# Column tiles of 32 for the attention sums of the second stage, a later split of the bias, and weight loads released after the first layer norm

## The reference, cut to what matters

```python
def attn(x, w_qkv, w_proj, b_proj):          # 16 heads of 64, 8 groups
    qkv = grouped_linear(x, w_qkv, None)
    q, k, v = (qkv[0] * D ** -0.5, qkv[1], qkv[2])
    attn = softmax(einsum('bhnd,bhmd->bhnm', q, k))
    out = einsum('bhnm,bhmd->bhnd', attn, v)
    return grouped_linear(out, w_proj, b_proj)

def ffn(x, w_gate, w_up, w_down):
    # _bitlinear: activations quantised to 8 bits per row, weights to -1, 0, 1
    # with the scale 1 / mean(|w|)
    gate = silu(_bitlinear(x, w_gate))
    up = _bitlinear(x, w_up)
    return _bitlinear(gate * up, w_down)

x = _layernorm(x + attn(x, w_qkv, w_proj, b_proj))
x = _layernorm(x + ffn(x, w_gate, w_up, w_down))
```

## Time and profile before

| | us |
|---|---|
| median of 3 runs | 1275.42 |
| lowest, highest | 1275.38, 1419.03 |
| the profiled execution | 1273.93 |
| its span (slowest core, core 7) | 1272.2 |
| spans of the eight cores | 1261.5 to 1272.2 |
| TensorE matmul busy | 1155.9 (91%) |
| VectorE busy | 907.3 (71%) |
| ScalarE busy | 581.4 (46%) |
| GpSimd busy | 232.1 (18%) |

### The profile page before, as it was taken

How to read it: one execution, slowest core, us unless ns; L and a number is a source line. 1 busy time by engine, 2 the same in 40 slices (tenths; PEclk the granted TensorE clock), 3 DMA queues, 4 the chain that set the end, 5 groups by cost and what they waited for, 6 DMA issues and landing times.

```text
span 1272.2 us, 17965 instructions; the slowest of 8 cores (1261.5 to 1272.2 us)
## 1 busy us (share of the span) xinstructions
PE 1155.9 (91%) x6502; PEld 453.8 (36%) x6502; DVE 907.3 (71%) x1748; ACT 581.4 (46%) x644; POOL 232.1 (18%) x236
## 2 busy tenths in 40 slices
PE   2898998886698879999999999999899999999997
PEld 0333332232232223333333333333444444444443
DVE  4788879998798786463746545444789777977774
ACT  2898997885354435554655556563011111111110
POOL 4132137764000862010101010000000000000000
PEclk9999998998898989999999999999999999999999
DMA  8999936699879594231423233110623333232303
GB/s 239 309 315 308 314 136 197 206 317 322 243 207 216 170 270 109 65 78 45 103 62 87 71 71 88 37 36 11 160 81 82 93 90 91 65 90 69 75 34 82
DMA packets 129895, 179.54 MB, mean 141 GB/s; under 512 B 90129, under 2 KB 90897, under 8 KB 129810
## 3 DMA queue, kind: packets, MB, share of 16 engines
q1 hardware_dynamic: 120338, 148.67, 41.6%
q0 software_dynamic: 8896, 29.27, 7.4%
q10 hardware_dynamic: 576, 0.46, 0.1%
HBM read 127.41 MB, written 30.93 MB: 124 GB/s over the span
## 4 chain that ended last, share of the span: by engine, by line
PE 66%; DVE 16%; DMA 8%; issue 4%; POOL 3%; ACT 3%; SPq 0%; POOLq 0%; DVEq 0%; ACTq 0%
PE ps L813 31%; PE ps L908 16%; PE ps L564 6%; PE ps L582 6%; DMA stage<-wu 5%; PE ps L589 5%; ACT P L570 2%; POOL G L434 2%; DVE wgq L450 2%; DVE asum L420 2%; DVE wuq L450 1%; DMA stage<-wd 1%; DMA xqT<-XQ 1%; DVE G L434 1%; DVE h L825 1%
## 5 line engine op out<-in xcount | busy, mean ns | idle before, releaser
L570 ACT ACTIVATE P<-ps 128x1024 bf16<-128x1024 f32 x512 | 493.1, 1023 | 260.7 <-PE ps L564 259.2
L813 PE MATMUL ps<-wgq,xqT 128*128 128x512 fp8e4 x1024 | 248.4, 382 | 26.8 <-DMA xqT<-XQ 17.5
L813 PE MATMUL ps<-wuq,xqT 128*128 128x512 fp8e4 x1024 | 251.7, 385 | 13.9 <-DVE h L825 13.9
L819 ACT ACTIVATE T<-ps,tsc 128x512 f32<-128x512 f32 x128 | 88.2, 689 | 385.0 <-PE ps L813 330.3
L908 PE MATMUL ps<-wdq,hqT 128*128 128x512 fp8e4 x1024 | 228.7, 379 | 0.0
L582 PE MATMUL ps<-P,onesb 128*64 128x512 bf16 x1024 | 206.5, 399 | 11.5 <-DVE DT L605 11.4
L589 PE MATMUL ps<-P,V 128*64 128x512 bf16 x1024 | 200.6, 388 | 1.0 <-DVE U L606 1.0
L564 PE MATMUL ps<-Q,K 64*128 64x512 bf16 x1024 | 175.0, 392 | 26.0 <-ACT P L570 13.2
L813 PEld LDWEIGHTS ps<-wgq,xqT 128*128 128x128 bf16 x1024 | 96.0, 98 | 156.7 <-issue 51.5
L813 PEld LDWEIGHTS ps<-wuq,xqT 128*128 128x128 bf16 x1024 | 96.7, 99 | 147.8 <-issue 42.4
L908 PEld LDWEIGHTS ps<-wdq,hqT 128*128 128x128 bf16 x1024 | 97.6, 98 | 126.0 <-issue 12.8
(11 more groups left out here) (95 smaller groups left out, 741.8 us busy)
## 6 DMA issues: line engine op xcount, KB each, us to landing
stage<-wu SPq DMA_DIRECT2D x64, 512.0 KB, 12.1
stage<-wd SPq DMA_DIRECT2D x58, 512.0 KB, 7.2
stage<-wg SPq DMA_DIRECT2D x42, 512.0 KB, 15.7
XB<-x SPq DMA_DIRECT2D x16, 512.0 KB, 4.6
xp_s<-XB SPq DMA_DIRECT2D x16, 512.0 KB, 2.6
Y<-xp_s SPq DMA_DIRECT2D x16, 512.0 KB, 3.9
y<-Y SPq DMA_DIRECT2D x16, 512.0 KB, 2.7
stage<-xT SPq DMA_DIRECT2D x10, 512.0 KB, 13.8
```

Of the source, the lines that this page charges most:

```text
L570: exp_tok[i] = act.do(lambda e: e.activation(P_sb[i % 4][:, :], bank(sb, 2), AF.Exp, bias=-C0, scale=0.125), pv_tok.get(i - 4), t)
L813: tp = pe.do(lambda e, ic=ic, w=w, bk=bk: e.matmul(bank(bk), xqT[b][:, ic, :], W_sb[w][:, 8 * q + ic, sl], start=(ic == 0), stop=(ic == 7) ...
L819: ta = act.do(lambda e: e.activation(T[:, :], bank(gb), AF.Tanh, bias=0.0, scale=tsc[:, t:t + 1]), tp, T_free[k], sc_tok[t])
```

## The change

1. The second piece of x for the first QKV units goes through the queue of SyncE, second in its order, and no longer through that of ScalarE.
2. The row of the bias is still loaded at the start, but `bias_rows` (the clearing, the five VectorE operations of one row, the two GpSimd DMAs) is emitted at i = 4 of the first stage's loop.
3. From step 256 on, `emit_pv_pair` replaces `emit_pv`. The outputs of a step are made with four matmuls on column tiles of 32 (two halves of each head). The denominators of two steps and two heads are made together with four matmuls on column tiles of 32: one 32-row quarter of bank 5 per head and parity of the step. Two steps take 12 matmuls instead of 8, and the order is outputs, outputs, denominators. `norm` then adds the two parities: four copies 32x16, one addition 128x16, and the reciprocal.
4. The first stage goes on to step 257 (three more rounds of its loop), and the second has 254 steps left.
5. `hold[0]` falls not at i = 230 but as soon as i > 244 and `bg` is empty, so behind `x2` of tile 0. The low credit of 0.3 from i = 242 on ends with it.
6. A limit of the down matrix costs 1.2 in the planner instead of 0.75, and up to three, not two, roundings may stand ahead of their limits.

```diff
-        t_x4[(g, j)] = (act if n == 1 else sp).dma(
+        t_x4[(g, j)] = sp.dma(
...
-    t = dve.do(lambda e: e.memset(b3[:, :], 0.0))
-    tb0 = sp.dma(sem("bias0"), bf[0:1, :], bproj_d[:, :])
...
-    t_b3 = bias_rows()
+    t_bias = sp.dma(sem("bias0"), bf[0:1, :], bproj_d[:, :])
...
-            if len(second) > 2:
+            if len(second) > (3 if w == 2 else 2):
                 yield limit()
...
-        return 0.75, None
+        return 0.75 if w < 2 else 1.2, None
...
+    def emit_pv_pair(i):
+        P, qc, kc = step_of(i)
+        buf = P % 2
+        first = kc == 0
+        last = kc == 14
+        for k in (i, i + 1):
+            for c in range(4):
+                t = pe.do(lambda e, k=k, c=c: e.matmul(
+                    ps[32 * c:32 * c + 32, 2048:2560], V_sb[buf][:, kc + k - i, 32 * c:32 * c + 32],
+                    P_sb[k % 4][:, 512 * (c // 2):512 * (c // 2) + 512],
+                    start=(first and k == i), stop=(last and k > i), tile_position=(0, 32 * c)),
+                    exp_tok[k], vt[(P, kc // 4)], u_done[0] if first else None,
+                    tick=(last and k > i and c == 3))
+        tu = t
+        for c in range(4):
+            h, k = c // 2, i + c % 2
+            t = pe.do(lambda e, c=c, h=h, k=k: e.matmul(
+                ps[32 * c:32 * c + 32, 2560:3072], onesb[:, 0:32],
+                P_sb[k % 4][:, 512 * h:512 * h + 512], start=first, stop=last,
+                tile_position=(0, 32 * c)), t_onesb, den_done[0] if first else None, tick=(c == 3))
...
+        if u >= 16:
+            for c in range(4):
+                d = 32 * (c ^ 1)
+                t2 = dve.do(lambda e, c=c, d=d: e.tensor_copy(
+                    RS[32 * c:32 * c + 32, :], DC[d:d + 32, :]), den_done[0])
+            t2 = dve.do(lambda e: e.tensor_tensor(RC[:, :], DC, RS[:, :], ALU.add), t2)
+            t2 = dve.do(lambda e: e.reciprocal(RC[:, :], RC[:, :]), t2)
...
-    for i in range(0, 252, 2):
+    for i in range(0, 258, 2):
...
+        if i == 4:
+            bias_rows()
...
-        if i == 230:
-            hold[0] = False
-            for s_ in range(22, 30):
-                stage_tok[s_] = t_qkv_last[0]
-            load_more()
...
-        att_weights(None if i < 242 else 0.3)
+        att_weights(None if i < 242 or not hold[0] else 0.3)
         if i > 244:
             bgstep(2.0)
+            if not bg and hold[0]:
+                hold[0] = False
+                for s_ in range(22, 30):
+                    stage_tok[s_] = t_qkv_last[0]
+                load_more()
```

More of the change, by code:

```diff
@@ L192, in build @@
     RC = alloc("RC", [128, 16], F32)[0]
+    RS = alloc("RS", [128, 16], F32)[0]
     ones, _ = alloc("ones", [128, 128], F32)
@@ L263, in build @@
             t_w[c] = t
-    t = dve.do(lambda e: e.memset(b3[:, :], 0.0))
-    tb0 = sp.dma(sem("bias0"), bf[0:1, :], bproj_d[:, :])
[L268 to L272, removed]
-    def bias_rows():
-        pool.dma(sem("bias1"), b3[1:2, :], bmid[0:1, :], tl)
-        return pool.dma(sem("bias1"), b3[2:3, :], blo[0:1, :])
-    t_b3 = bias_rows()
+    t_bias = sp.dma(sem("bias0"), bf[0:1, :], bproj_d[:, :])
+    def bias_rows():
+        t = dve.do(lambda e: e.memset(b3[:, :], 0.0))
+        t = dve.do(lambda e: e.tensor_copy(b3[0:1, :], bf[0:1, :]), t, t_bias)
+        t = dve.do(lambda e: e.tensor_tensor(bf[0:1, :], bf[0:1, :], b3[0:1, :], ALU.subtract), t)
+        t = dve.do(lambda e: e.tensor_copy(bmid[0:1, :], bf[0:1, :]), t)
+        t = dve.do(lambda e: e.tensor_tensor(bf[0:1, :], bf[0:1, :], bmid[0:1, :], ALU.subtract), t)
+        t = dve.do(lambda e: e.tensor_copy(blo[0:1, :], bf[0:1, :]), t)
+        pool.dma(sem("bias1"), b3[1:2, :], bmid[0:1, :], t)
+        t_b3[0] = pool.dma(sem("bias1"), b3[2:3, :], blo[0:1, :])
+    t_b3 = [None]
     t_wproj = pool.dma(sem("wproj"), wproj_sb[:, :], wproj_d[:, :])
@@ L597, in emit_pv @@
             norm(2 * P + qc, td, t)
+    def emit_pv_pair(i):
[18 more added lines that the diff above has]
+                tile_position=(0, 32 * c)), t_onesb, den_done[0] if first else None, tick=(c == 3))
+        pv_tok[i] = pv_tok[i + 1] = t
+        last_pv[P] = t
+        if last:
+            norm(2 * P + qc, t, tu)
     def norm(u, td, tu):
@@ L608, in norm @@
         free[4] = [u_done[0]]
-        t2 = dve.do(lambda e: e.reciprocal(
-            RC[:, :], DT[:, :].rearrange("r (k c) -> r k c", c=32)[:, :, 0]), den_done[0])
+        DC = DT[:, :].rearrange("r (k c) -> r k c", c=32)[:, :, 0]
+        t2 = den_done[0]
+        if u >= 16:
[5 more added lines that the diff above has]
+            t2 = dve.do(lambda e: e.reciprocal(RC[:, :], RC[:, :]), t2)
+        else:
+            t2 = dve.do(lambda e: e.reciprocal(RC[:, :], DC), t2)
         t3 = dve.do(lambda e: e.transpose(
@@ L659, in att_steps @@
                 emit_st(i + 2 + k)
+        if i >= 256:
+            emit_pv_pair(i)
         for k in range(n):
             now[0] += 1
-            emit_pv(i + k)
+            if i < 256:
+                emit_pv(i + k)
             ast[0] += 1
@@ L731, in proj_half @@
         pe.do(lambda e: e.matmul(bank(bk), onesb[:, :], b3[:, 512 * hf:512 * hf + 512],
-                                 start=True, stop=False), t_onesb, t_b3, *free[bk], tick=False)
+                                 start=True, stop=False), t_onesb, t_b3[0], *free[bk], tick=False)
         for j in range(4):
@@ L1024, in build @@
                 while ast[0] < NSTEP:
-                    att_steps(1)
+                    att_steps(2)
                 while later:
```

## The result

The changed kernel takes 1256.3 us (median of 4 runs, 1255.45 to 1342.58) against 1275.4 for the kernel before in the same measurement: ratio 0.985, 95% interval 0.9828 to 0.9873. That is 19 us faster. Forecast were 1225 us, 50 less, with a range of 1203 to 1258. The measured time lies at the slow end of the range, and the gain is well under half of what was forecast, so the working was wrong somewhere, not only rough. The prediction gave 0.82 to a gain of more than 2%; it is 1.5%.

A forecast was written before the change was run, and what follows sets the result against it. Bounds taken by stretch: DMA loads, VectorE's down-matrix sums, GpSimd roundings and loads, then TensorE's passes from 488 to 890 us. 1273.9 - 23.5 + 2 - 22 - 6 - 2 + 3 - 2 = 1223.4, median 1225; range 1203 to 1258.

The forecast's parts named there:

- tiles of 32 (with two pairs fewer): Full stretch: a pair of attention steps takes 1.40 us, not 1.62, and 92 pairs replace 94; -23.5 us.
- the longer norm: Five more small VectorE operations per norm: nothing for twelve in the full stretch, +2 us for two in the VectorE-bound stretch.
- planner of the down limits: Stretch before the first down product: limits spread over 43 ticks, not 26, taking 73 us, not 95; -22 us.
- end of the first stage (-6 -2 +3): Before the first gate product: faster transpose -6, shorter up loads -2, later down-matrix loads +3 us.
- start: Kernel start: first exp 13 us earlier, mostly given back to waits on loads; -2 us, ends -13 and +3.
- (b): Rival for the attention tiles: four column tiles half as parallel, 0.43 us a pass, 1302 us in all; chance 0.08.
- (c): Rival for the attention tiles: concurrency with loss, 0.27 us a pass of four, 1243 us in all; chance 0.12.
- TensorE alone: Lower bound for the stretch up to the first down product: 49 ticks at 1.33 us, 65 us.
- The transpose term: First XQ transpose, before the first gate product: 3.1 us, not 9.0, with fewer down-matrix loads beside it; -6 us.
- They cost nothing as long as that chain is longer: Six added first-stage steps run free beside layer norm and transpose, needing 5.8 us of ScalarE and 4.9 of TensorE.
- (d): Rival for the kernel start: the earlier start counts in full, -13 us not -2, 1214 us in all; chance 0.12.
- (a): Rival for the down-matrix sums: GpSimd and loads still pace the roundings, -5 us not -22, 1242 in all; chance 0.12.

The follow-up runs named there:

- the second profile: The changed kernel itself, unaltered, profiled in a second measurement; ratio to the kernel before 0.9854.
- The run with the waiting background jobs: The changed kernel, with no background job of VectorE emitted in the four ticks from a norm on; ratio to the kernel before 0.9766.
- the run of parts 4 and 5 alone: The kernel before with only the three added first-stage rounds and the later release of the slots; ratio 1.000.
- the run with i = 0: The changed kernel with the bias split emitted at i = 0, ahead of the first sum, instead of i = 4; ratio to the kernel before 0.9839.

## Why the prediction was wrong, point by point

That 1256 lies inside the range is luck: the range was made wide for the rivals, and four of the terms were off, three of them by about 8 us or more. By its own signs the prediction was wrong: the first down product starts at 497.3 (it named 495 as the limit; 493.4 in the second profile), and the first gate product at 324.6, not 317 to 321. Two steps at 1.41 us, the first exp at 11.1 and a transpose of 3.2 to 4.0 us came as written.

| term | forecast, us | measured alone, us |
|---|---|---|
| tiles of 32 (with two pairs fewer) | -23.5 | -21.7 |
| the longer norm | +2 | +13.8 |
| planner of the down limits | -22 | -13.5 |
| end of the first stage (-6 -2 +3) | -5 | 0 |
| start | -2 | +1 |
| sum | -50.5 | -20.4 |

The first line mixes two things. Of its -23.5, 94 x 0.22 = 20.7 are the tiles, and 2 x 1.40 = 2.8 the two pairs that parts 4 and 5 take out of the full stretch. Put where they belong, the forecasts are -20.7 for the tiles (measured -21.7) and -7.8 for parts 4 and 5 (measured 0). Of the 30 us missing, the norm is 11.8, the planner 8.5, the end of the first stage 7.8 and the start 3.

**The tiles.** Right in mechanism and size. The pair costs 1.41 us, a pass of four 0.22. Rivals (b) and (c) are out. With the tiles and without the additions the full stretch is 18.0 us shorter with 1.9 more idle, 19.9 us, which is 94 pairs at 0.21. That TensorE's saving is worth nothing in the stretch that VectorE holds was right too (179.1 and 179.5 us from gate to down). The Trainium skill's page "TensorE: Matmul & The Clock Gate" (Measured speedup vs the span model) has both numbers. Two passes of four take 0.45 us here, 0.225 each, so its 4 ns for each further tile, 12 ns a pass, fits; the loss that the prediction worked out from its 2.38x for three tiles, 0.27 us a pass, does not show.

**The norm: the step that failed most.** "Twelve fall into the full stretch, where VectorE is busy 201.5 of 381.8 us and TensorE idle 2.3 us in all: nothing there, 14 us if each delay came through." The duration was right (four copies 0.75 us, addition 0.18, the whole about 1.1 us), and the upper bound of 14 us was nearly the value, 13.8 alone and 14.5 in the changed kernel. That the two figures agree so closely is chance: the 14 us was the work passed on in full, and in the full stretch most of the norms stall nothing, and two of them cost 6.5 and 5.5 us. What was wrong is the reason for zero: a mean load of 53% was taken for slack. VectorE works in order; its jobs come in chains, a norm of 3.3 us and a layer norm's of about 4.2, and the bank that TensorE needs next is emptied behind them. When two chains meet, the excess comes through, and more, as the granted clock is lower after the wait. The run with the waiting background jobs shows it: nearly the same work, 10.6 us back in the full stretch.

**The planner.** -22 was forecast with a bound at -10, -13.5 came. The wait of VectorE for GpSimd went (13.5 us to 2.3 us), as written. The step that failed is "TensorE alone" as the thing that is late next: of the 73 us taken for the last 49 ticks, VectorE's work was never added up. It was 146.5 of 181 us from first gate to first down before, 156.2 of 174.3 after. That sum would have pointed to VectorE and not TensorE as what takes over; the waits of the changed kernel say so.

**The end of the first stage.** The transpose term came nearly in full: alone, parts 4 and 5 let it land 3.2 to 3.5 us after its issue on all cores (7.8 to 9.6 before), at 321.0 in place of 326.7 by the medians. But before, the first gate product started 0.2 to 0.3 us behind the landing; now it starts 1.4 to 1.7 us behind it, so 4.4 us of 5.7 reach it. In the changed kernel the transpose is also issued 2 us later than before (319.8 and 317.7), lands at 323.1, and the gate product follows at 324.6. What stands between is this, on core 6, the latest of them. Timeline after:

```profile
321.94 0.71 DVE L633 STREAM_TRANSPOSE DT<-ps 128x512 f32<-128x512 f32 x1
...
322.21 1.35 SPq L78 DMA_TRANSPOSE xqT<-XQ  x1
...
322.57 0.65 DVE L634 COPY U<-ps 128x512 f32<-128x512 f32 x1
...
323.37 1.04 PE L609 MATMUL ps<-P,V 128*32 128x512 bf16 x8 [3.81 <-DVE U L634]
...
327.10 1.02 PE L854 MATMUL ps<-wgq,xqT 128*128 128x512 fp8e4 x4 [0.45 <-DVE XB L782]
```

"They cost nothing as long as that chain is longer": step 256 opens a new block of 16, so its first sum needs the banks emptied by the norm of step 255, which stands on VectorE behind the layer norm. TensorE waits 3.81 us, and P1 and the gate product are queued behind it, 0.9 us later than the transpose's landing (4.0 us after its issue) on this core. The added steps became the end of the chain, at a price of 1 to 2 us. And the up load took 16.90 us after and 16.55 before: the eight loads less did not shorten it. The failed steps are thus the free run of the added steps and the -2 of the up loads; the larger loss, the 2.8 us by which the full stretch grows in the run of parts 4 and 5 alone, has no term in the prediction, and its cause was not tested.

**The start.** Right in the main point (first exp 11.4 us earlier by the medians, none of it kept), and the -2 was +1, which is not apart from nothing. The prediction named the cost as an end of its range (+3, "the bias's 6.3 us now lie between QKV copies"), and the DMA share of the run with i = 0 shows that place as its cause. Rival (d) is out.

**The rivals and the range.** None of the four is what happened. (a) had the right place for 8.5 of the 30 us that are missing, but the wrong engines. The case that was missing is: VectorE in order behind longer chains. Its price stood in the text, "14 us if each delay came through", and got no chance of its own.

## What to carry to other kernels

For an engine that works in order and empties a bank for another one, the mean load does not tell the slack: add up the longest chain that can stand ahead of the emptying operation, and compare it with what the other engine has to do meanwhile. Five operations of 0.2 us, 16 times, cost 14 us here, and keeping the two chains four ticks apart brought 11 back.
When an edit takes one wait away, add up the next engines' work in that stretch before giving the stretch to the fastest of them. And work hidden in a wait must lie inside it: the same six operations cost 1 to 5 us less inside the 13 us before the first tile than one place later, and 7 us more ahead of the one value that all roundings wait for.

## What the runs showed of the hardware that was not expected

After each of the two waits of TensorE, of 3.57 and 3.81 us, with products back to back before and behind it, the granted clock was below full for some microseconds, where it was 1.00 in all of the earlier trace rows from 488 to 890: the products stood for a while at the lower of its two levels, 1.2 and not 2.4 GHz. Behind the first wait four products take 1.86 us in place of 1.04, and so on until 684.8; 10 us at a mean of 0.75 are 2.5 us lost, and some more lies in the slice before. Behind the second, eight products take 3.18 us in place of 1.89 and the next four 1.46, 1.7 us more. The two stalls so cost about 6.5 and 5.5 us: 12 of the 13 us that the full stretch lacks. The slices in question:

```profile
680.00:690.00 10.00, 10.00 (x56) 3.04 (x55) 3.46 (x10) 4.45 (x5) 0.00 (x0) 0.75 0.37 133
745.90:750.00 4.10, 4.08 (x12) 1.52 (x12) 1.55 (x3) 0.69 (x1) 0.19 (x1) 0.58 0.99 281
```
